# TensorE's heads 2 to 31 as loops of six, three places for x and three banks for z, in a state-space convolution with a LoRA layer behind it

## The reference, cut to what matters

```python
# x: (128, 32, 512): 128 sequences, 32 heads, 512 positions
K = 2 * Re(einsum('hn,hnl->hl', Ct, exp(dtA * l)))        # 32 kernels of 512 taps
y = irfft(rfft(x, 1024) * rfft(K, 1024))[..., :512]       # a causal convolution
x = x + (y + x * D[:, None]) * (l < length)               # masked by sequence length
A, Bw = lora_A_w[ids], lora_B_w[ids]                      # one adapter per sequence
x = x + x @ base_weight.T + base_bias + (x @ A.T) @ Bw.T
```

## Time and profile before

| | |
|---|---|
| median of 3 runs | 210.38 us (210.12 to 210.66) |
| the profiled execution's own time | 210.57 us |
| its span, first to last instruction | 208.5 us |
| mean granted TensorE clock | 1.000 |
| convolution, first to last matmul | 21.35 to 86.29 us |
| HBM read, written | 45.64 MB, 10.65 MB |

### The profile page before, as it was taken

How to read it: one execution, slowest core, us unless ns; L and a number is a source line. 1 busy time by engine, 2 the same in 40 slices (tenths; PEclk the granted TensorE clock), 3 DMA queues, 4 the chain that set the end, 5 groups by cost and what they waited for, 6 DMA issues and landing times.

```text
span 208.5 us, 4394 instructions
## 1 busy us (share of the span) xinstructions
PE 190.8 (91%) x1063; PEld 166.4 (80%) x1063; DVE 168.1 (81%) x368; ACT 120.9 (58%) x354; POOL 90.3 (43%) x144
## 2 busy tenths in 40 slices
PE   0049999999999999899999999999999999999994
PEld 0037999999999899787888888888888888888883
DVE  3985598789799976877999978788888878888662
ACT  2798974343736446237767656657566565656530
POOL 4850000001356778085564645546455464545500
PEclk9999999999999999999999999999999999999999
DMA  5973999999999999983767666677776676765324
GB/s 141 400 310 105 377 410 409 409 413 406 412 411 407 409 407 422 339 262 105 257 238 247 217 207 228 214 201 224 213 222 204 216 229 201 218 200 186 103 101 151
DMA packets 21520, 56.46 MB, mean 271 GB/s; under 512 B 3266, under 2 KB 3970, under 8 KB 21250
## 3 DMA queue, kind: packets, MB, share of 16 engines
q1 hardware_dynamic: 18002, 47.55, 62.2%
q0 software_dynamic: 2560, 8.39, 13.3%
q10 hardware_dynamic: 944, 0.36, 0.7%
HBM read 45.64 MB, written 10.65 MB: 270 GB/s over the span
## 4 chain that ended last, share of the span: by engine, by line
PE 87%; DMA 6%; DVE 4%; POOL 1%; issue 1%; DVEq 0%
PE z_ps L932 26%; PE y_ps L971 20%; PE k_ps L971 20%; PE z_ps L959 7%; DMA strip<-k_pad 5%; PE y_ps L904 3%; PE y_ps L998 2%; PE y_ps L997 2%; PE k_ps L998 2%; PE k_ps L997 2%; PE k_ps L913 1%; DMA par<-params 1%; PE y_ps L1020 1%; PE k_ps L1020 1%; PE y_ps L981 1%
## 5 line engine op out<-in xcount | busy, mean ns | idle before, releaser
L932 PE MATMUL z_ps<-xp,strip 128*128 128x512 f32 (+3 forms) x384 | 63.4, 326 | 0.3 <-DMA strip<-k_pad 0.3
L932 PEld LDWEIGHTS z_ps<-xp,strip 128*128 128x128 f32 x384 | 59.3, 196 | 4.3 <-DMA strip<-k_pad 0.4
L417 POOL DMA_INDIRECT b_hl<-b_tab,b_idx x32 | 37.7, 1178 | 15.3 <-issue 8.5
L412 POOL CAST ag<-a_hl 128x128 fp32r x64 | 23.3, 367 | 41.0 <-PE z_ps L959 30.4
L971 PE MATMUL y_ps<-w_hi,xp 128*128 128x512 f32 x120 | 39.5, 390 | 0.0
L971 PE MATMUL k_ps<-w_hi,xp 128*128 128x512 f32 x120 | 39.5, 390 | 0.0
L550 ACT ACTIVATE ag<-a_hl 128x64 fp32r x128 | 25.6, 249 | 20.5 <-issue 20.3
L462 ACT ACTIVATE xp<-z_all 128x512 fp32r<-128x512 f32 x32 | 19.7, 627 | 19.7 <-PE z_ps L932 18.2
L741 DVE TENSOR_TENSOR xp<-z_all,xp 128x512 fp32r<-128x512 f32 x32 | 26.5, 827 | 5.3 <-ACT xp L462 5.2
L971 PEld LDWEIGHTS y_ps<-w_hi,xp 128*128 128x128 f32 x120 | 22.5, 188 | 4.3
L971 PEld LDWEIGHTS k_ps<-w_hi,xp 128*128 128x128 f32 x120 | 22.5, 188 | 4.2
(11 more groups left out here) (138 smaller groups left out, 239.4 us busy)
## 6 DMA issues: line engine op xcount, KB each, us to landing
strip<-k_pad SPq DMA_DIRECT2D x31, 512.0 KB, 7.9
z_all<-x_conv SPq DMA_DIRECT2D x16, 512.0 KB, 8.5
x_t<-x_tile SPq DMA_DIRECT2D x32, 256.0 KB, 2.8
out<-a_raw SPq DMA_DIRECT2D x31, 256.0 KB, 2.4
a_raw<-a_t SPq DMA_DIRECT2D x2, 512.0 KB, 8.3
x_t<-b_rows SPq DMA_DIRECT2D x2, 512.0 KB, 8.8
w_sb<-w_t SPq DMA_DIRECT2D x2, 512.0 KB, 10.0
b_tab<-b_hl SPq DMA_DIRECT2D x1, 1024.0 KB, 10.1
```

Of the source, the lines that this page charges most:

```text
L412: last = g.tensor_copy(ag[:, s, :, :, q, :].rearrange("p c e r -> p e c r"), src)
L417: g.indirect_dma_start(out=b_hl[:, t % BS, :].bitcast(F32), out_offset=None, in_=b_tab, in_offset=bass.IndirectOffsetOnAxis(ap=b_idx[:, t: ...
L932: last = nc.tensor.matmul(z_ps[:, h % ZS, m * P:L], strip[:, h % SS, m * P:(m + 1) * P, t], xp[:, h % XS, 0:LC - m, e, :], start=(n == 0), ...
```

## The change

- TensorE: heads 0 and 1 stand alone (`first_head`); heads 2 to 31 are five rounds of `six_heads`. A loop of two rounds has `late_group` behind each (groups 2 and 3, after heads 7 and 13), a loop of three has none. The waits in them are for values that a register gives.
- x has three places (`x_slot`: 1 to 3) and z three banks (`z_bank`: 1 to 3) instead of four. ACT's split of x and TensorE's wait for the mask count from head h-3, VectorE masks head h-3 beside head h. Place 0 of `xp` and bank 0 of `z_ps` are left to the tiles.
- Groups 2 and 3 both use slot 0 of `gg`, `ee`, `k_ps` and `k_sb`. Their D is added by VectorE (`k_first_lag`) before ACT rounds.
- Strip 1 is loaded in two halves, as strip 0 is.
- 12 warm matmuls instead of 15 and 2.
- x's pair 15 moves behind strip 25, the second half of the weights behind strip 27.
- x tile 2 is loaded before the tables of B, x tile 3 before the bias.
- ACT takes `h_down(0)` before `x1_hi(2)`; VectorE takes tile 0's h before tile 2's remainder, and `h_remainder(0)` before `x1_of(3)`.
- GpSimd's iota, mask and clearing work starts behind group 1's factors, not behind group 0's.

```diff
-X_AT = {7: 8, 10: 9, 13: 10, 15: 11, 18: 12, 20: 13, 22: 14, 24: 15}
+X_AT = {7: 8, 10: 9, 13: 10, 15: 11, 18: 12, 20: 13, 22: 14, 25: 15}
-A_AT, B_AT, W_AT = {9: 0, 12: 1}, {17: 0, 19: 1}, {24: 0, 26: 1}
+A_AT, B_AT, W_AT = {9: 0, 12: 1}, {17: 0, 19: 1}, {24: 0, 27: 1}
-K_AFTER = {2: 7, 3: 14}
-WARM_0, WARM_1 = 15, 2
+K_AFTER = {2: 7, 3: 13}
+K_SLOT = (0, 1, 0, 0)
+WARM_0 = 12
...
+        def x_slot(h):
+            return (h + 1) % CS + 1
+        def z_bank(h):
+            return h % CS + 1
...
-                if h == 0:
-                    load_strip(h, 0, 0, L // 2, strip_begun)
-                    load_strip(h, 0, L // 2, L, strip_landed[0])
+                if h < 2:
+                    load_strip(h, h, 0, L // 2, strip_begun[h])
+                    load_strip(h, h, L // 2, L, strip_landed[h])
...
             load_x_tile(1, 1)
+            load_x_tile(2, 2)
             store_table(0, b_hl[:, :, :].bitcast(F32), tab_hi_stored)
             store_table(1, b_lo, tab_lo_stored)
+            load_x_tile(3, 3)
             sp.dma_start(bias_sb[:, :], bias.to_broadcast((P, L))).then_inc(bias_in, 16)
-            load_x_tile(2, 2)
-            load_x_tile(3, 3)
...
-            pool.wait_ge(factors, 2)
+            pool.wait_ge(factors, 2 * KS)
...
-                if h >= XS:
-                    act.wait_ge(conv_done, h + 1 - XS)
+                if h >= CS:
+                    act.wait_ge(conv_done, h + 1 - CS)
...
                 act.wait_ge(k_done, k + 1)
+                if k in K_AFTER:
+                    act.wait_ge(d_added, 1 + list(K_AFTER).index(k))
...
+            h_down(0, 0)
             x1_hi(2, 2, True)
-            h_down(0, 0)
...
+            def k_first_lag(k):
+                (h0, h1), s = GROUPS[k], K_SLOT[k]
+                dve.wait_ge(k_done, k + 1)
+                lag_0 = k_ps[0:1, s, 0:(h1 - h0) * NC:NC]
+                V.tensor_tensor(lag_0, lag_0, d_sb[:, h0:h1], ALU.add).then_inc(d_added, 1)
...
-            for h in range(XS, NH):
-                head(h - XS)
+            for h in range(CS, NH):
+                head(h - CS)
                 for k, last in K_AFTER.items():
-                    if h == last + XS:
+                    if h == last + CS:
+                        k_first_lag(k)
                         k_low(k)
...
             x1_of(2, 2, 0)
+            h_masked(0, 0)
             x1_remainder(2, 2)
-            h_masked(0, 0)
+            h_remainder(0, 0)
             x1_of(3, 3, 0)
-            h_remainder(0, 0)
...
+            def late_group(lap):
+                k0, k1 = K_AFTER
+                pe.wait_ge(factors, lap * 2 + 2 * (k0 + 1))
+                pe.wait_ge(k_lo_done, lap * (before(k1) - before(k0)) + before(k0) + 1)
+                group(None, K_SLOT[k0], G)
...
+            def six_heads(lap):
+                for s in range(2, SS + 2):
+                    pe.wait_ge(strip_landed[s % SS], 16 * (lap + (s // SS + 1)))
+                    pe.wait_ge(xc_lo_done, lap * SS + (s + 1))
+                    pe.wait_ge(z_masked, lap * SS + (s - 1))
+                    products(s)
...
-            group(0)
+            early_group(0)
             pe.wait_ge(xc_hi_done, 1)
             keep_warm(WARM_0)
-            group(1)
-            keep_warm(WARM_1)
-            for h in range(NH):
-                head(h)
-                for k, last in K_AFTER.items():
-                    if h == last:
-                        group(k)
+            early_group(1)
+            first_head(0)
+            first_head(1)
+            with pe.Fori(0, len(K_AFTER)) as lap:
+                six_heads(lap)
+                late_group(lap)
+            with pe.Fori(len(K_AFTER), NH // SS) as lap:
+                six_heads(lap)
```

More of the change, by code:

```diff
@@ L61 @@
 ZS = 4
+CS = 3
 KS = 2
@@ L86 @@
 BC = AD * R // NW
-assert BC == P and G * (NA + NL) == L and NW == LC == XT and EARLY % XS == TS
+assert BC == P and G * (NA + NL) == L and NW == LC == XT and SS % CS == 0 and NH % SS == 2
 def build(nc, x_conv, x_tile, params, table, d_row, length, ids_all, w_t, bias, a_t, b_rows, out):
@@ L188, in build @@
         tab_hi_stored, tab_lo_stored = sem("tab_hi_stored"), sem("tab_lo_stored")
-        k_stored, pad_stored, strip_begun = sem("k_stored"), sem("pad_stored"), sem("strip_begun")
+        k_stored, pad_stored, strip_begun = sem("k_stored"), sem("pad_stored"), [sem(f"strip_begun{n}") for n in range(2)]
         pool_step, dve_step = sem("pool_step"), sem("dve_step")
@@ L211, in build, with turn_of, before @@
         base_done, y_done, o_done = sem("base_done"), sem("y_done"), sem("o_done")
+        def turn_of(k):
+            return sum(K_SLOT[j] == K_SLOT[k] for j in range(k + 1))
+        def before(k):
+            return max(j for j in range(k) if K_SLOT[j] == K_SLOT[k])
+        def x_slot(h):
+            return (h + 1) % CS + 1
+        def z_bank(h):
+            return h % CS + 1
         def in_chunks(a):
@@ L459, in split_x @@
                 act.wait_ge(x_landed[h // XP], 16)
-                if h >= XS:
-                    act.wait_ge(conv_done, h + 1 - XS)
-                act.activation(xp[:, h % XS, :, 0, :], z_all[:, h, :, :], ACT.Copy).then_inc(xc_hi_done, 1)
+                if h >= CS:
+                    act.wait_ge(conv_done, h + 1 - CS)
+                act.activation(xp[:, x_slot(h), :, 0, :], z_all[:, h, :, :], ACT.Copy).then_inc(xc_hi_done, 1)
             def group_sines(k):
@@ L470, in group_store @@
             def group_store(k):
-                (h0, h1), s = GROUPS[k], k % KS
+                (h0, h1), s = GROUPS[k], K_SLOT[k]
                 n = h1 - h0
                 act.wait_ge(k_done, k + 1)
+                if k in K_AFTER:
+                    act.wait_ge(d_added, 1 + list(K_AFTER).index(k))
                 if k >= KS:
-                    act.wait_ge(k_stored, 16 * (k + 1 - KS))
+                    act.wait_ge(k_stored, 16 * (before(k) + 1))
                 if k >= 1:
@@ L703, in multiply @@
                     if k >= KS:
-                        dve.wait_ge(k_done, k + 1 - KS)
+                        dve.wait_ge(k_done, before(k) + 1)
                     both = ct[:, :, h0:h1].rearrange("p o h -> p h o").unsqueeze(3).to_broadcast((P, n, 2, NA))
@@ L746, in head @@
                 dve.wait_ge(conv_done, h + 1)
-                V.tensor_tensor(z_all[:, h, :, b0:b1], in_chunks(z_ps[:, h % ZS, :])[:, :, b0:b1], mask[:, :, b0:b1],
+                V.tensor_tensor(z_all[:, h, :, b0:b1], in_chunks(z_ps[:, z_bank(h), :])[:, :, b0:b1], mask[:, :, b0:b1],
                                 ALU.mult).then_inc(z_masked, 1)
@@ L773, in _ @@
             remainder(2)
-            remainder(3)
             beside = {h: do for k, at in STEPS_AT.items() for h, do in zip(at, group(k))}
-            for h in range(XS, NH):
-                head(h - XS)
+            for h in range(CS, NH):
+                head(h - CS)
                 for k, last in K_AFTER.items():
-                    if h == last + XS:
+                    if h == last + CS:
+                        k_first_lag(k)
                         k_low(k)
@@ L855, in part_of_remainder @@
                                 by_head(xp[:, t, :, 0, :].bitcast(F32), h0, h1), ALU.subtract).then_inc(done, 1)
-            for h in range(NH - XS, EARLY):
+            for h in range(NH - CS, EARLY):
                 head(h)
@@ L903, in keep_warm, with group @@
                 for _ in range(n):
-                    nc.tensor.matmul(y_ps[:, 0, :], xp[:, 0, 0, 0, :], xp[:, 0, :, 0, :], start=True, stop=True)
-            def group(k):
-                (h0, h1), s = GROUPS[k], k % KS
+                    nc.tensor.matmul(y_ps[:, 0, :], xp[:, x_slot(0), 0, 0, :], xp[:, x_slot(0), :, 0, :], start=True, stop=True)
+            def group(k, s, n):
+                for i in range(n):
+                    last = nc.tensor.matmul(k_ps[0:NA, s, i * NC:(i + 1) * NC], gg[:, s, i, :], ee[:, s, i, :],
+                                            start=(i == 0), stop=(k is None and i == n - 1))
+                if k is None:
+                    last.then_inc(k_done, 1)
+                else:
+                    h0, h1 = GROUPS[k]
+                    nc.tensor.matmul(k_ps[0:NA, s, 0:n * NC:NC], row0[:, :], d_sb[:, h0:h1],
+                                     start=False, stop=True).then_inc(k_done, 1)
@@ L909, in group, with early_group @@
+            def early_group(k):
+                h0, h1 = GROUPS[k]
                 pe.wait_ge(factors, 2 * (k + 1))
                 if k >= KS:
[L911 to L926, removed]
+                    pe.wait_ge(k_lo_done, before(k) + 1)
+                group(k, K_SLOT[k], h1 - h0)
+            def late_group(lap):
[3 more added lines that the diff above has]
+                group(None, K_SLOT[k0], G)
@@ L927, in head, with products @@
+            def products(s):
                 terms = [(m, t, e) for m in range(LC) for t, e in ((0, 0), (0, 1), (1, 0))]
```

(10 more changed lines are left out.)

8 lines of the change are left out of this document (4 added, 4 removed).

## The result

The changed kernel takes 213.55 us in the median of four runs (213.29 to 213.69); the kernel before takes 210.27 in the median of four (210.12 to 210.66). The ratio is 1.0149, 95% interval 1.0137 to 1.0161: slower by 3.1 us by this ratio, by 3.3 by the medians, where +0.8 was forecast; it lies above the forecast's whole range (209.5 to 212.6). The profiled execution took 213.63 for a span of 211.5, against 208.5.

What follows compares the result with a forecast made beforehand. It took TensorE, busy 91% of the span, as the bound, with only the first 98 us movable. Convolution +0.9 and transition -0.1 gave +0.8 us: 211.4, or 211.2 on the median's scale, range 209.5 to 212.6.

Steps and rivals of the forecast that it cites:

- the third and fourth group: Groups 2 and 3 in the convolution: TensorE stands 0.8 us at the former and 1.65 us at the latter.
- the one-stall rival: Third group costs the start's gain, fourth finds VectorE nearly caught up: no change, 210.4 us; chance 0.08.
- The D product's removal and VectorE's add: Groups 2 and 3: TensorE's 0.70 us becomes about 0.6; VectorE's add takes 0.2, bounds 0.1 to 0.4.
- The DMA wait at 72.38 vanishes: Head 25 no longer waits for its strip, taking 0.4 us off the lateness.
- The last part's -0.35: Tile 0's h first and x tile 2 before the tables: -0.35 us, bounds -0.24 to -0.5.
- The adapter ids: VectorE's ids at head 20 have one head less in reserve: 0 to 0.3 us more, taken as 0.
- It is wrong if heads in the loops take more than 1.96 us each: Sign against the forecast: looped convolution heads taking longer than 1.96 us each.
- Strip 2, 0 to 0.3 us of delay, taken as 0.1: Head 2's strip comes one issue later: 0 to 0.3 us of delay, taken as 0.1.
- The loops themselves, nothing: Loop branches in the convolution priced at nothing; without cover each would cost at least 0.228 us.
- The transition, +0.25: From last heads to tiles: ACT's later weight rounding delays VectorE's last mask by 0.25 us, down to 0.
- VectorE did not keep pace: Rival that VectorE keeps pace, so TensorE never stands at groups 2 and 3: faster, 209.4 us; chance 0.18.
- The branches: Rival: three loop jumps fetch code anew, 1.3 us each, up to 3.9 us: 213 to 215 us; chance 0.08.

Runs made afterwards that it cites:

- experiment 1: Changed kernel with TensorE waiting for the mask of head h-3 in place of head h-2; ratio 1.0047 to the kernel before.
- experiments 10: Kernel before with the change's last part, its earlier start and its order of loads, strip 1 whole, written out; ratio 0.9957 to the kernel before.
- experiment 11: Kernel before with everything of the change except loops, places, banks and D, so strip 1 in halves; ratio 0.9965 to the kernel before.
- experiment 6: Changed kernel, looped, with the wait for head h-3's mask, and the groups' steps and ACT's weight rounding one head earlier; ratio 0.9987 to the kernel before.
- experiment 12: Changed kernel with all of ACT's side roundings (A, B, weights) one head earlier; 212.08 us, ratio 1.0076 to the kernel before.
- Experiments 3: Changed kernel with strip 1 loaded whole again instead of in halves; ratio 1.0117 to the kernel before.
- experiment 7: Changed kernel, rounds written out, with head h-3's mask wait, and the groups' steps and ACT's weight rounding one head earlier; ratio 0.9985 to the kernel before.
- experiment 2: Changed kernel with VectorE's six steps of groups 2 and 3 one head earlier; ratio 1.0031 to the kernel before.
- 13: Changed kernel with ACT's side roundings and the groups' steps one head earlier, and the wait for head h-3's mask; ratio 0.9975 to the kernel before.
- experiment 5: Changed kernel with only ACT's rounding of the weights one head earlier; ratio 1.0132 to the kernel before.
- experiment 4: Changed kernel with the five rounds of six heads written out instead of looped; ratio 1.0088 to the kernel before.

## Why the prediction was wrong in size

**The direction and the third and fourth group: right.** "It stands 0.8 us" at group 2 measured 0.74. Both groups stood, so the one-stall rival is out too. For group 3, head 8 to head 15 was forecast to take 16.0 us and took 15.8, though split otherwise: 0.98 of stand, and 0.37 that the mask waits had already spread over heads 8 to 13 (experiment 1). The D product's removal and VectorE's add: the add takes 0.16 us, forecast 0.2. "The DMA wait at 72.38 vanishes", 0.4, measured 0.45 (+3.27 at head 20 to +2.82 at the end). Here that is no test of the reason, because TensorE came to head 25 at 75.22, so late that no strip could hold it; experiments 10 and 11 show that the reason holds. The last part's -0.35 measured -0.35 (+3.37 to +3.02), and alone it is worth a ratio of 0.9983.

**The adapter ids "with one head less in reserve, 0 to 0.3 more, taken as 0": wrong, 0.92 of idle.** This is the largest miss. The step assumed a wait for head h-3's mask. The wait is for head h-2's, and VectorE takes that only after the ids. Experiment 1 removes the idle and 1.1 us from head 14 on. With the wait I had assumed, experiment 1 shows no idle and experiment 6 0.23 us, both inside my bounds, so the step failed in the number of buffers that the wait leaves. The second condition, a cast that is long beside GpSimd, is nothing that the change brought (1.32 us before, 1.35 after), but without it the wait costs nothing at head 20 (experiment 12). The same wait cost about 0.06 us a head in heads 8 to 13 (12.10 against 11.73 for six). "It is wrong if heads in the loops take more than 1.96 us each" thus came true by a little: these take 1.99 us from start to start, the kernel before's 1.97.

**"Strip 2, 0 to 0.3 us of delay, taken as 0.1", with head 0 at 20.5: wrong, 0.7.** Head 0 started at 20.75 and head 2 at 25.15 instead of 24.44. Strip 2 landed at 24.92, 0.6 us later than before (24.32), and the loop added 0.2 behind it. I had taken the quickest landing of the list for the first strip, and the spacing of later strips for strip 2. Experiments 3, 10 and 11 show that strips 1 and 2 take back half a microsecond or more of the start in either form: with strip 1 in halves strip 2 landed between 24.41 and 25.28, with strip 1 whole between 24.32 and 24.62, but then head 1 waits. Since the groups' factors count from head 4, this shift went through to the groups in full. What makes strip 2 land at 24.41 in one execution (experiment 7) and at 25.28 in another (experiment 2) I didn't settle.

**"The loops themselves, nothing": wrong where TensorE had stood.** The trace of before had jumps only behind a running queue. My own forecast put the two jumps behind stands of 0.8 and 1.65 us, and did not ask what a jump costs with nothing queued: 0.29 and 0.17 us more than written out, and 0.2 at head 2. Where TensorE had not stood, experiments 6 and 7 have 0.13 and 0.07. By the Trainium skill, "Runtime: NRT & Kernel Launch", section Instruction fetch mechanics, the danger of a jump is a page fetched anew; the packet counts show none fetched here, and what the jumps cost is the sequencer's own work, a branch of up to 0.23 us and three register instructions.

**The transition, +0.25: measured +0.55.** I counted ACT's lateness, not that GpSimd's work on the weights would now run beside VectorE's sums, 2.40 us for 1.23. Experiments 12 and 13 return the 1.23, and with it and the repairs the idle is 0.71. My bounds for the transition, -0.35 to +0.3, also don't follow from its terms, whose own bounds give -0.5 to 0; it measured +0.2. How much of the rest is ACT's loads of the adapters' numbers stays open: the idle of ACT between gathers was 0.35 to 1.1 us in the changed kernel, and up to 1.75 in experiment 5.

**The rivals.** VectorE did not keep pace. The branches cost a sixth of that rival's 3.9 us, by another mechanism.

## What to carry to other kernels

When unrolled work becomes a loop, work out the value of each wait for one round, at its first and last head: a value held positive by one more count may ask for one buffer less than there is. Whether it costs anything then depends on how long the partner's other work takes at that place. Side work bound to an index ("beside head 9") moves in time when the number of buffers changes; move its index with it. The tile loop's jumps cost nothing behind long matmuls, but behind a group of sixteen short ones a jump cost 0.07 to 0.13 us, and 0.17 to 0.29 where TensorE had stood; price it again at every such place.

## What was not expected of the hardware

A conversion on VectorE that began beside a GpSimd tensor operation ended only 0.11 us after it: 1.35 us against 0.23 with GpSimd idle. In the ten traces of this study where the two overlap it takes 1.32 to 1.35 us, in the five others 0.23. VectorE's sums of two arrays in SBUF took 2.40 us for two beside GpSimd's subtraction and 1.23 without it. A TensorE head in a loop began 0.23 us after its strip's landing where TensorE had run dry, and 0.04 us after it written out (24.74 to 24.78 in experiment 4, 24.78 to 24.82 in experiment 11).
